# Layer 1 attention: low parts of six k halves on VectorE instead of GpSimd

## What is computed

```python
B, T, D = (2, 256, 256)
H, G, DQ, DV = (16, 4, 128, 128)      # 16 query heads, 4 groups of k and v
...
N, t, _ = hidden_states.shape
q = (hidden_states @ Wq).reshape(N, t, H, DQ).transpose(0, 2, 1, 3)
k = (hidden_states @ Wk).reshape(N, t, G, DQ).transpose(0, 2, 1, 3)
v = (hidden_states @ Wv).reshape(N, t, G, DV).transpose(0, 2, 1, 3)
q = _rope(q)
k = _rope(k)
k = jnp.repeat(k, REP, axis=1)
v = jnp.repeat(v, REP, axis=1)
scores = jnp.einsum('bhtd,bhsd->bhts', q, k)
scores = scores + _alibi(t)[None]
scores = scores / math.sqrt(DQ)
scores = 30.0 * jnp.tanh(scores / 30.0)
causal = jnp.tril(jnp.ones((t, t), bool))
scores = jnp.where(causal[None, None], scores, -jnp.inf)
probs = jax.nn.softmax(scores, axis=-1)
ctx = jnp.einsum('bhts,bhsd->bhtd', probs, v)
ctx = ctx.transpose(0, 2, 1, 3).reshape(N, t, H * DV)
return ctx @ Wo + bo
```

## Time and profile before

| what | us |
|---|---|
| median of 3 runs | 838.12 |
| lowest and highest | 834.84, 838.96 |
| the profiled execution | 838.65 |
| its span, first to last instruction | 836.9 |
| TensorE busy (matmul) | 790.9 (95%) |
| VectorE busy | 607.8 (73%) |
| ScalarE busy | 466.2 (56%) |
| GpSimd busy | 424.0 (51%) |

### The profile page before, as it was taken

How to read it: one execution, slowest core, us unless ns; L and a number is a source line. 1 busy time by engine, 2 the same in 40 slices (tenths; PEclk the granted TensorE clock), 3 DMA queues, 4 the chain that set the end, 5 groups by cost and what they waited for, 6 DMA issues and landing times.

```text
span 836.9 us, 14053 instructions
## 1 busy us (share of the span) xinstructions
PE 790.9 (95%) x4927; PEld 645.2 (77%) x4927; DVE 607.8 (73%) x1077; ACT 466.2 (56%) x822; POOL 424.0 (51%) x479
## 2 busy tenths in 40 slices
PE   6999999998889889998999999999999999999997
PEld 5777777765433367797999889989999999988885
DVE  8588869648989968778888688887767654445556
ACT  4433242359888833687656456655666655655431
POOL 1757846613554446455345433758565512655540
PEclk9999999999999999999999999999999999999999
DMA  5211186000000040000000000102010587743207
GB/s 186 69 45 38 39 255 182 1 1 1 1 1 2 1 129 26 26 7 26 7 20 7 8 20 7 58 26 65 21 51 26 200 200 266 279 149 104 57 2 251
DMA packets 50116, 59.82 MB, mean 71 GB/s; under 512 B 13559, under 2 KB 41084, under 8 KB 50048
## 3 DMA queue, kind: packets, MB, share of 16 engines
q1 hardware_dynamic: 45488, 50.49, 19.7%
q0 software_dynamic: 4560, 8.44, 2.8%
HBM read 41.11 MB, written 21.86 MB: 75 GB/s over the span
## 4 chain that ended last, share of the span: by engine, by line
PE 54%; DVE 11%; POOL 6%; ACT 6%; issue 4%; DMA 3%; SPq 0%; POOLq 0%; ACTq 0%; DVEq 0%
PE ps L802 12%; PE ps L517 8%; PE ps L519 8%; PE ps L518 8%; PE ps L895 4%; PE ps L926 3%; PE ps L892 3%; POOL A L1818 2%; DVE cap L1511 2%; DVE swap L1500 2%; PE ps L713 2%; PE ps L874 1%; DMA xa<-xg_scratch 1%; PE ps L559 1%; ACT A L1109 1%
## 5 line engine op out<-in xcount | busy, mean ns | idle before, releaser
L802 PE MATMUL ps<-V,P 128*128 128x129 f32 x1152 | 151.0, 277 | 0.0
L1161 ACT ACTIVATE cap<-cap 128x1024 f32<-128x1024 f32 (+7 forms) x128 | 87.3, 682 | 112.4 <-DVE cap L1511 106.9
L802 PEld LDWEIGHTS ps<-V,P 128*128 128x128 f32 x1152 | 143.6, 192 | 2.7
L1511 DVE SCALAR_TENSOR_TENSOR cap<-dist,ps 128x1024 f32<-128x1024 f32 (+7 forms) x128 | 95.4, 750 | 26.3 <-PE ps L519 22.9
L1742 POOL TENSOR_SCALAR_AFFINE_SELECT P<-P 128x128 f32<-128x128 f32 x128 | 39.4, 308 | 143.2 <-ACT P L1166 142.7
L1874 POOL DMA_INDIRECT y_scratch<-y_sb,aux_s x63 | 62.1, 985 | 61.8 <-issue 33.1
L1166 ACT ACTIVATE P<-cap 128x1024 f32<-128x1024 f32 (+7 forms) x128 | 87.9, 687 | 4.1
L517 PE MATMUL ps<-q_hi,k_hi 128*128 128x512 f32 x192 | 72.1, 376 | 6.8 <-DVE cap L1511 6.2
L519 PE MATMUL ps<-q_lo,k_hi 128*128 128x512 f32 x192 | 67.3, 351 | 0.0
L518 PE MATMUL ps<-q_hi,k_lo 128*128 128x512 f32 x192 | 66.9, 349 | 0.0
L517 PE MATMUL ps<-xT_hi,w_hi 128*128 128x512 f32 x128 | 56.4, 441 | 2.9 <-POOL w_lo L1762 1.9
(11 more groups left out here) (293 smaller groups left out, 2100.6 us busy)
## 6 DMA issues: line engine op xcount, KB each, us to landing
xg_scratch<-blank SPq DMA_DIRECT2D x1, 8127.0 KB, 31.2
xa<-xg_scratch SPq DMA_DIRECT2D x63, 128.0 KB
ew<-in_experts SPq DMA_DIRECT2D x3, 1920.0 KB, 8.9
y<-y_scratch SPq DMA_DIRECT2D x8, 512.0 KB
pk<-in_packed SPq DMA_DIRECT2D x8, 384.0 KB, 3.1
pks<-in_scales SPq DMA_DIRECT2D x8, 384.0 KB, 4.0
ew<-in_experts SPq DMA_DIRECT2D x1, 3072.0 KB
wqk<-in_wqk SPq DMA_DIRECT2D x20, 128.0 KB
```

The source lines that it names most:

```text
L802: last = pe.matmul(ps[:, 4 + r % 2, o:o + D1 + 1], P1[:, h % 2, a:a + P], V1[:, j, h // REP, :], start=(j == 0), stop=(j == t))
L1161: act.activation(cap[:, CAP_AT[j]:CAP_AT[j] + w], cap[:, CAP_AT[j]:CAP_AT[j] + w], ACT.Tanh, scale=1.0 / (CAP * float(D1) ** 0.5))\
L1511: dve.scalar_tensor_tensor(out=cap[:, CAP_AT[j]:CAP_AT[j] + w], in0=dist[:, 0:w], scalar=slope, in1=psf[:, 1024 * (n % 2):1024 * (n % 2) + ...
```

## The change

The low parts of the k halves of groups 1, 2 and 3 (`LATE_K`, six halves) are no longer taken by GpSimd. VectorE takes them with a new step `k_low`, which `follow` puts behind the scores step that is two steps after the one beside which the half was projected: behind the cap of j = 4 for heads 1, 5, 9, behind that of j = 2 for heads 2, 6, 10. The step waits for the high part (`parts_hi`) and counts a new semaphore `k_low_ready`, for which TensorE waits before the first scores of heads 4, 8 and 12. `by_pool` counts how many low parts GpSimd has made; VectorE's own wait before it writes a `rot` buffer again is dropped where the low part is its own. Both halves of group 0 stay on GpSimd.

```diff
@@ tensor
             def scores1(h, j):
                 n = h * NT + j
                 if j == 0:
-                    pe.wait_ge(parts_ready, part_of["project", PROJ.index(("q", h)), 1] + 1)
+                    pe.wait_ge(parts_ready, by_pool(part_of["project", PROJ.index(("q", h)), 1]))
+                    if h >= REP and h % REP == 0:
+                        pe.wait_ge(k_low_ready, 2 * (h // REP))
@@ vector
                 k = part_of["project", n, half]
-                if k >= 3:
-                    dve.wait_ge(parts_ready, k - 2)
+                if k >= 3 and PROJ[PARTS[k - 3][1]] not in LATE_K:
+                    dve.wait_ge(parts_ready, by_pool(k - 3))
...
+            def k_low(n, half):
+
+                k = part_of["project", n, half]
+                tk = slice(half * HALF, (half + 1) * HALF)
+                g = PROJ[n][1]
+                dve.wait_ge(parts_hi, k + 1)
+                dve.tensor_tensor(k_lo[:, g % 2, tk], rot[:, k % 3], k_hi[:, g % 2, tk].bitcast(F32), ALU.subtract)\
+                    .then_inc(k_low_ready, 1)
@@ gpsimd
             def project_part(n, half):
                 kind, hd = PROJ[n]
+                if PROJ[n] in LATE_K:
+                    return
@@ the order
+PARTS = [s for s in STEPS1 if s[0] == "project"]
+part_of = {s: n for n, s in enumerate(PARTS)}
+LATE_K = [("k", g) for g in range(1, G1)]
+
+
+def by_pool(k):
+
+    return sum(1 for s in PARTS[:k + 1] if PROJ[s[1]] not in LATE_K)
...
         if name == "scores":
             out.append(s)
+            if lows and lows[0][0] <= NT * s[1] + s[2]:
+                out.append(("k_low", *lows.pop(0)[1:]))
...
+            if engine == "dve" and PROJ[s[1]] in LATE_K:
+                at = [x for x in STEPS1[:n] if x[0] == "scores"][-1]
+                lows.append((NT * at[1] + at[2] + 2, *s[1:]))
```

More of the change, by code:

```diff
@@ L410, in build_program @@
         pj_ps, pj_cos, pj_rot = sem("pj_ps"), sem("pj_cos"), sem("pj_rot")
-        parts_hi, parts_ready = sem("parts_hi"), sem("parts_ready")
+        parts_hi, parts_ready, k_low_ready = sem("parts_hi"), sem("parts_ready"), sem("k_low_ready")
         s1_ps, s1_bias, s1_exp, s1_mask = sem("s1_ps"), sem("s1_bias"), sem("s1_exp"), sem("s1_mask")
@@ L1702, in _ @@
                  "values": values, "logits": logits, "turn_logits": turn_logits, "router": router,
-                 "ranks": ranks, "moe": moe, "turn_x": layernorm_lo}[step[0]](*step[1:])
+                 "ranks": ranks, "moe": moe, "turn_x": layernorm_lo, "k_low": k_low}[step[0]](*step[1:])
             for s in range(MOE_EARLY, NBLK + 2):
@@ L1950 @@
 side_of = {s: n for n, s in enumerate(SIDE)}
-part_of = {s: n for n, s in enumerate([s for s in STEPS1 if s[0] == "project"])}
+PARTS = [s for s in STEPS1 if s[0] == "project"]
[3 more added lines that the diff above has]
+    return sum(1 for s in PARTS[:k + 1] if PROJ[s[1]] not in LATE_K)
 def follow(engine):
-    out, later, held = [], [], []
+    out, later, held, lows = [], [], [], []
     for n, s in enumerate(STEPS1):
```

## The result

The changed kernel takes **841.82 us**, the median of 13 runs (839.68 to 845.30), against 837.0 us for 13 runs of the kernel before (833.97 to 841.85): a ratio of 1.0062 with a 95% interval of 1.0045 to 1.0079, some 5.2 us slower (the medians themselves lie 4.8 us apart). The profiled execution took 839.68 us.

A forecast was written before the change was run, and what follows sets the result against it. TensorE was taken to bound layer 1's attention (334 to 690 us). First halves 3.4 plus second halves 2.6 gave 6.0 us, added to the profiled execution's difference and median 838.12: 844.1 us, range 839.0 to 848.7.

The forecast's parts named there:

- First halves: Heads 1, 5, 9: k_low waits for k_hi, delaying VectorE's work that TensorE awaits; +1.3, +0.8, +1.3, together 3.4 us.
- Second halves, heads 6 and 10: k_low, both inputs in SBUF, is stretched by GpSimd's rot and delays TensorE's output projection; +1.0 us each.
- Head 2: Second half: 1.05 us for k_low, 0.45 given back because GpSimd runs ahead and L1553's stretch can shrink; +0.6 us.
- the port is lost twice: Rival, chance 0.08: k_low at heads 2, 6, 10 behaves like L1634, about 1.2 us more at two; 846.5 us.
- The clock fell once more: Rival, chance 0.2: head 9's longer wait makes TensorE's clock fall to half, costing 1.7 us; 845.8 us.
- Covered: Rival, chance 0.12: VectorE's idle time at heads 1, 5, 9 absorbs k_low, only the second halves cost; 840.7 us.
- The port conflicts dissolve: Rival, chance 0.09: VectorE's router operations regain 4.3 us lost to GpSimd, against 3.7 for six k_low; 837.5 us.
- k_lo itself was waited for: Rival, chance 0.03: each handover saves 0.6 us because VectorE is quicker, 3.6 in all; 834.5 us.

The follow-up runs named there:

- removed version: Against the kernel before: no engine takes the low parts of k for groups 1 to 3, their scores read group 0's; 835.31 us, ratio 0.9989.
- second profile of before: The unchanged kernel before, run and profiled again beside the experiments; 834.48 us, one run.
- first halves alone: Against the kernel before: only the first halves (heads 1, 5, 9) go to VectorE, the second stay on GpSimd; 840.84 us, ratio 1.0062.
- late: Against the changed kernel: all six subtractions on VectorE moved behind the cap of j = 7 of their head; 835.21 us, ratio 0.999 against before.
- spread: Against the changed kernel: first halves moved behind the cap of j = 5, second halves behind j = 7; 836.78 us, ratio 1.0014 against before.
- mixed: Five low parts on VectorE behind the cap of j = 7, head 5's left to GpSimd; 834.57 us, ratio 0.9998 against before.
- wait-only: Against the kernel before: GpSimd keeps all low parts, VectorE only waits for k_hi at the first halves' places; 839.47 us, ratio 1.0056.
- one-half versions: Against the kernel before: only first halves moved to VectorE, 840.84 us, ratio 1.0062; or only second halves, 838.43 us, ratio 1.0026.

## Why the prediction was right, and where it was off

It said 844.1 us and slower; it is 841.8 and slower. Of the 2.3 us between, 1.1 is the base (838.12 was the median of 3 runs, 13 runs give 837.0) and 0.8 the terms, 6.0 against 5.2; 0.4 is left, by which the medians (4.8 us apart) differ from the heads (5.2), and no run separates it. The terms:

| term | forecast | measured |
|---|---|---|
| head 1, first half | 1.3 | 1.28 |
| head 5, first half | 0.8 | 0.56 |
| head 9, first half | 1.3 | 1.01 |
| head 2, second half | 0.6 | 0.04 |
| head 6, second half | 1.0 | 0.99 |
| head 10, second half | 1.0 | 0.97 |
| head 3 | none | 0.34 |
| sum | 6.0 | 5.2 |

The sum is nearer than its terms deserve, and that part is luck: heads 2 and 3, put at 0.6, came to 0.38 only because an unforeseen 0.34 stood in for most of what head 2 did not cost.

- **First halves.** The mechanism was right at all three: idle time ahead of k_low, ended by k_hi (2.65, 2.65, 3.30 us), 0.69 us long, TensorE waiting at j = 7. The size at heads 5 and 9 was off because I took k_hi's time over from before. With VectorE waiting, nothing stands in GpSimd's way: at head 5 rot, 1.46 us beside the router's comparison before, is free of it, and k_hi comes 0.2 us earlier, counted from the head's start, as it does at head 9, where wqk_lo shrinks from 0.93 to 0.73 us. The wait partly makes its own cause shorter.
- **Second halves, heads 6 and 10.** k_low is 1.08 us beside GpSimd's rot:

```profile
466.13 1.08 DVE L1511 TENSOR_TENSOR k_lo<-rot,k_hi 128x512 fp32r<-128x512 f32 x1
```

```profile
465.36 1.31 POOL L1860 TENSOR_TENSOR rot<-rot,swap 128x512 f32<-128x512 f32 x1
```

  It ends at 467.21, 0.54 us behind rot (466.67); the forecast was 0.56 behind, from L1634.
- **Head 2.** The term that was mis-sized is the relief. I gave back 0.45 us; the removed version puts it at 0.9, and k_low, at 1.26 us longer than the 1.05 I had costed, cost next to nothing net. The reason that I gave for it is wrong too: L1553's stretch did go, from 1.39 to 0.42, but the operation ahead of it grew from 0.29 to 1.11 us. The rest comes from a later router operation (L1560 before, L1571 after), which fell from 1.38 to 0.42. VectorE of the second profile of before, then of the kernel after, then GpSimd:

```profile
378.80 0.29 DVE L1552 TENSOR_SCALAR scr<-scr 128x256 f32<-128x256 f32 x1
379.12 1.41 DVE L1553 TENSOR_TENSOR scr<-scr 128x256 f32<-128x256 f32 x1
...
385.28 1.38 DVE L1560 TENSOR_TENSOR scr<-scr 128x256 f32<-128x256 f32 x1
```

```profile
374.85 1.26 DVE L1511 TENSOR_TENSOR k_lo<-rot,k_hi 128x512 fp32r<-128x512 f32 x1
...
379.56 1.11 DVE L1563 TENSOR_SCALAR scr<-scr 128x256 f32<-128x256 f32 x1
380.70 0.42 DVE L1564 TENSOR_TENSOR scr<-scr 128x256 f32<-128x256 f32 x1
...
385.86 0.42 DVE L1571 TENSOR_TENSOR scr<-scr 128x256 f32<-128x256 f32 x1
```

```profile
374.82 0.74 POOL L1833 TENSOR_TENSOR wqk_lo<-wqk,wqk_hi 128x256 fp32r<-128x256 f32 x1 [0.55 <-ACT wqk_hi L1127]
375.52 1.73 POOL L1860 TENSOR_TENSOR rot<-rot,swap 128x512 f32<-128x512 f32 x1
```

  k_low ends 0.55 us behind wqk_lo (375.56) and not behind rot, though rot's record starts at 375.52, before k_low ends. I read this as VectorE getting in between two GpSimd operations, and rot took 1.73 us in place of some 1.3. The rival "the port is lost twice" thus did not happen at any of the three. The Trainium skill, SBUF — State Buffer, section Who interferes with whom, calls the shared ports an exclusive lock; by that the two durations are explained together, and the trace agrees (k_low 1.26 us, rot 1.73). Who gets them when both engines wait, these rows show for this place only.
- **Head 3**, +0.34 us, I did not see; see the last section.
- **The clock fell once more** (0.2) was half right: behind head 9's wait it fell in 2 of 5, for 1.6 us. What I left out is that the change also ends falls at heads 2 and 3, so that on average its clock is a little better, not worse.
- **Covered** falls with the first halves alone, which cost TensorE 2.8 us over all three places. **The port conflicts dissolve** falls with the removed version, in which the relief is worth 0.9 us. **k_lo itself was waited for** falls with the removed version too, in which 0.9 us is all that can be had.
- Three figures of the prediction are off without changing the result. GpSimd is 8.3 us less busy in the stage (184.05 to 175.76), not 7.7. The first k_low pair is done some 35 us before head 4 begins (376.1 against 411.1), not 10, so that cover is safer than I said. And the sum, one fall of the clock and one lost port give 848.2 us by the prediction's own terms, not 848.7.
- Of the stage 334 to 690 us I said it would be some 6 us longer. Between the two first profiles it is 333.05 against 331.03 us by heads, because before's held two falls of the clock. The test was badly chosen: a length of that size is only readable with the falls counted.

## What to carry to other kernels

A step moved to an in-order queue costs what it holds up: its wait and its own duration, less the slack of what stands behind. Here 0.6 us of work cost 1.3 us ahead of a cap that TensorE needed, and nothing three caps later, behind j = 7, at the same head. Look for the place where its input is long ready and no other engine waits for what follows, before asking which engine is quicker. Compare short repeated pieces (a head, a layer) over several profiles of each kernel, since one event of the clock is larger than the effect sought.

## What the hardware did that I had not expected

- **VectorE can start late for no listed reason.** The 0.34 us at head 3 lie ahead of one cT_lo. In the kernel after ScalarE's cT_hi ends at 403.27 and VectorE starts at 403.72, 0.45 us later; in the second profile of before 403.65 and 403.75. ScalarE, then VectorE, kernel after:

```profile
402.69 0.58 ACT L1175 ACTIVATE cT_hi<-ps 128x512 fp32r<-128x512 f32 x1
```

```profile
403.72 0.69 DVE L1543 TENSOR_TENSOR cT_lo<-ps,cT_hi 128x512 fp32r<-128x512 f32 x1 [2.89 <-ACT cT_hi L1175]
```

  and VectorE, second profile of before:

```profile
403.75 0.69 DVE L1532 TENSOR_TENSOR cT_lo<-ps,cT_hi 128x512 fp32r<-128x512 f32 x1 [2.54 <-ACT cT_hi L1173]
```

  It is 0.45 to 0.46 in all four profiles of after, in late, spread and mixed, and 0.10 to 0.11 in three of before and in the removed, wait-only and one-half versions: a property of the kernel, not of the execution. The seven carry five or six k_low steps on VectorE, the others three or none. The cause is not shown; no experiment was made on it.
- **A fall of the clock is not decided by the length of the wait alone.** The same kernel with the same 2.1 us wait at head 9 has it or not (0.51 against 1.00 above), while a wait of 2.1 us at head 2 had it 4 times in 4. What differs between two executions stays open.
- **The experts' stage varies by itself.** From head 15 to the end it took 172.51, 169.20, 169.46 and 169.90 us in four executions of after, 170.31, 170.77 and 169.58 in three of before. That is up to 3.3 us between executions of one kernel, and with the falls of the clock it is one reason why medians of the small versions (late, mixed) can't be told from before.
